# The inverse's X on the other partition half: four quarters of the array in place of two, and an order of work that has level products first

## What is computed

```
mem = 0.9 * mem + sd_t;  spike = sigmoid(10 * (mem - 0.5)) in the gradient, (mem > 0.5) in value
mem = mem - spike * 0.5
alpha = sigmoid(ab_t + alpha_spike * spike);  beta = sigmoid(bb_t + sum(spike * beta_spike))
alpha = 1 and beta = 0 where no key channel of the head spikes
s = s * alpha[:, None];  u = k_t @ s
s = s - beta * outer(k_t, u) + beta * outer(k_t, v_t)
out_t = s^T q_t
```

## Time and profile before

| | |
|---|---|
| median of 3 runs | 1183.43 us (1169.3 to 1190.45) |
| the profiled execution | 1186.2 us, span 1184.5 us |
| mean granted TensorE clock | 0.956 |
| PE busy | 1079.8 us (91%), 17266 matmuls |
| PEld busy | 769.0 us (65%) |
| DVE busy | 701.1 us (59%) |
| ACT busy | 519.5 us (44%) |
| POOL busy | 200.7 us (17%) |

### The profile page before, as it was taken

How to read it: one execution, slowest core, us unless ns; L and a number is a source line. 1 busy time by engine, 2 the same in 40 slices (tenths; PEclk the granted TensorE clock), 3 DMA queues, 4 the chain that set the end, 5 groups by cost and what they waited for, 6 DMA issues and landing times. The chain is left out here.

```text
span 1184.5 us, 41088 instructions
## 1 busy us (share of the span) xinstructions
PE 1079.8 (91%) x17266; PEld 769.0 (65%) x17266; DVE 701.1 (59%) x2517; ACT 519.5 (44%) x1500; POOL 200.7 (17%) x390
## 2 busy tenths in 40 slices
PE   7878789999999999999999997898999999899987
PEld 3332278888888888888888884456456456545642
DVE  2887868888878888887776551244336225323610
ACT  7566213444444444444444343144254245325411
POOL 7100101122122122212211201211103001110200
PEclk8999759999999999999999898899999999899999
DMA  2000000000000000000000003100000000000000
GB/s 89 1 1 1 1 2 3 5 4 4 4 4 4 4 5 4 4 4 4 4 27 4 4 4 101 31 1 1 0 9 10 1 9 1 10 1 1 10 1 9
DMA packets 12805, 11.38 MB, mean 10 GB/s; under 512 B 1563, under 2 KB 11407, under 8 KB 12623
## 3 DMA queue, kind: packets, MB, share of 16 engines
q1 hardware_dynamic: 12623, 8.75, 2.5%
HBM read 7.70 MB, written 1.05 MB: 7 GB/s over the span
## 5 line engine op out<-in xcount | busy, mean ns | idle before, releaser
L1220 ACT COPY work<-banks 128x128 f32<-128x128 f32 x160 | 42.8, 268 | 168.8 <-PE banks L926 168.8
L892 PE MATMUL banks<-work 64*64 64x64 f32 x3072 | 102.6, 232 | 6.7 <-DVE gates L599 5.8
L926 PE MATMUL banks<-work,gates 64*64 64x32 f32 x2560 | 105.3, 221 | 3.1 <-issue 2.8
L946 PE MATMUL banks<-work 64*64 64x32 f32 x2560 | 105.5, 223 | 0.4 <-ACT work L1220 0.4
L203 DVE SCALAR_TENSOR_TENSOR mom<-gates 128x16 f32<-128x16 f32 x512 | 101.3, 198 | 5.8
L926 PEld LDWEIGHTS banks<-work,gates 64*64 64x64 f32 x2560 | 93.5, 139 | 15.4 <-issue 11.4
L599 DVE COPY_PREDICATED gates<-work,banks 128x256 f32<-128x256 uint32 x192 | 101.9, 531 | 1.1
L199 DVE SCALAR_TENSOR_TENSOR gates<-mom,gates 128x16 f32<-128x16 f32 x512 | 96.7, 189 | 9.6 <-ACT gates L1193 4.5
L604 DVE TENSOR_TENSOR work<-work,banks 128x128 f32<-128x128 f32 x128 | 36.8, 288 | 101.1 <-PE banks L936 99.9
L936 PEld LDWEIGHTS banks<-work 64*64 64x64 f32 x2048 | 74.2, 139 | 32.9 <-issue 22.3
L946 PEld LDWEIGHTS banks<-work 64*64 64x64 f32 x2560 | 92.2, 139 | 0.5 <-ACT work L1220 0.5
(11 more groups left out here) (235 smaller groups left out, 2348.9 us busy)
## 6 DMA issues: line engine op xcount, KB each, us to landing
qT<-in_x_dram SPq DMA_DIRECT2D x4, 256.0 KB, 4.3
work<-in_x_dram SPq DMA_DIRECT2D x4, 256.0 KB, 4.0
out_dram<-work SPq DMA_DIRECT2D x4, 256.0 KB, 3.1
gates<-in_w_ff_dram SPq DMA_DIRECT2D x3, 256.0 KB, 3.1
wv_sb<-in_wv_dram SPq DMA_DIRECT2D x1, 512.0 KB, 4.9
work<-in_w_out_dram SPq DMA_DIRECT2D x1, 512.0 KB, 5.3
gates<-in_x_Wq_dram SPq DMA_DIRECT2D x1, 512.0 KB, 5.9
gates<-in_x_Wk_dram SPq DMA_DIRECT2D x1, 512.0 KB, 6.6
```

The source lines that it names most:

```text
L892: last = pe.matmul(level_out(l)[to, a], KS[rows, n.two, hp], late[rows, hp], start=True, stop=True)
L926: last = pe.matmul(packed(psZX, l)[rows, hp], EA[rows, n.three, l, hp], first_half(X, l)[rows, hp], start=True, stop=True)
L946: last = pe.matmul(packed(psXT, l)[rows, hp], Z[rows, l - 1, hp], second_half(XT[:, n.two], l)[rows, hp], start=True, stop=True)
L1220: ac.copy(first_half(Z[:, l - 1], l), packed(psZX, l)).then_inc(z_ok, 1)
```

## The change

X, Z, XT, EA and res of a head get places of their own (`at_x`, `at_z`, `at_xt`, `at_level`, `at_res`), such that make_z, make_x, turn_start and solve read one partition half and write either one, two heads for each quarter of the array. make_xt and read_chunk stay within a half. Matmuls from the two halves must not write one bank at once, so X's and Z's products are spread over banks 6 and 7 (`psZX = paired(6)`), and XT's products move to the second half of bank 5, where the spike counts were. The counts move to free columns of the level products' bank 0, by a matmul of their own, `spike_counts`. Since that bank is then read by alpha and beta, levels 1 and 3 wait for these, and alpha moves behind keep of level 0. make_xt waits for the ScalarE operations that read bank 5. The copy that starts XT becomes three copies (two of them move a half to the other).

The order within a step: TensorE does level ahead of xt, with spike_counts and spike_sums of l = 4 around that level (before, both were at the end of l = 3). VectorE does add_xt behind keep, and drive one place earlier.

The core of the diff (the index changes of the other matmul loops are of the kind shown for make_z; `counts`, `counts_as` and the like give the counts' place):

```diff
-        psZX, psXT = bank[6], bank[7]
+        psZX = paired(6)
+        psZX_half = psZX[:, :, 0:W]
+        psXT = psG[:, B * C:B * C + HP * W].rearrange("p (a n) -> p a n", a=HP)
...
+        def counts(g):
+            if g.n <= HP:
+                return psG[:, B * C:2 * B * C]
+            return psL[:, 0:2, 2 * C:4 * C]
...
+        by_time = [(par, 2 * t + (t + swap) % 2) for par in range(2) for swap in range(2) for t in range(2)]
+        by_parity = [(par, 2 * t + (par + swap) % 2) for t in range(2) for swap in range(2) for par in range(2)]
...
+        def at_level(par, hp):
+            return head_rows[hp // 2], 2 * par + (hp // 2 + hp) % 2
+
+        def at_x(par, hp):
+            return head_rows[hp // 2], 2 * (hp % 2) + par
+
+        def at_z(par, hp):
+            return head_rows[hp % 2], 2 * (hp // 2) + par
+
+        def at_xt(par, hp):
+            return head_rows[hp % 2], 2 * ((hp // 2 + hp) % 2) + par
+
+        def at_res(par, hp):
+            return head_rows[hp % 2], 2 * par + hp // 2
 
...
                 def alpha(g):
                     ve.wait_ge(al0_ok, g.n + 1)
-                    ve.scalar_tensor_tensor(g.tokens(aT[:, g.hp]), by_chunk(psG[:, B * C:2 * B * C]), 0.0, by_chunk(al0),
-                                            ALU.is_equal, ALU.max).then_inc(alpha_ok, 1)
+                    ve.wait_ge(count_mm, g.n + 1)
+                    ve.scalar_tensor_tensor(by_chunk_as(g, g.tokens(aT[:, g.hp])), counts_by_chunk(g), 0.0,
+                                            by_chunk_as(g, by_chunk(al0)), ALU.is_equal, ALU.max).then_inc(alpha_ok, 1)
 
                 def beta(g):
...
                             add_x(nxt, l)
                         spike(scan, h + 1)
-                        if nxt:
-                            add_xt(nxt, l)
                         spike(scan, h + 2)
                         if aft:
                             prefix(aft, l)
@@ -676,6 +713,10 @@
                         spike(scan, h + 4)
                         if aft:
                             keep(aft, l)
+                        if nxt:
+                            add_xt(nxt, l)
+                        if l == 4 and gate:
+                            drive(gate)
                         spike(scan, h + 5)
                         if l == 1 and gate:
                             spikes(gate)
@@ -683,16 +724,12 @@
                             beta(gate_old)
                         if l == 3 and aft2:
                             scale_key(aft2)
-                        if l == 4 and gate:
-                            drive(gate)
                         if l == 4 and aft2:
                             scale_query(aft2)
                     spike(scan, 6 * NINV)
                     if cur:
                         update(cur, 0)
                         update(cur, 1)
-                    if gate:
-                        alpha(gate)
                     if aft2:
                         prefix(aft2, 0)
                         suffix(aft2, 0)
@@ -700,6 +737,8 @@
                     if aft2:
                         diagonal(aft2)
                         keep(aft2, 0)
+                    if gate:
+                        alpha(gate)
                     if cur and cur.it == ROUNDS - 2:
                         scale_out()
 
...
+                def level(n, l, gate=None, gate_old=None):
+                    if l == 1 and gate_old:
+                        pe.wait_ge(alpha_ok, gate_old.n + 1)
+                    if l == 3 and gate_old:
+                        pe.wait_ge(beta_ok, gate_old.n + 1)
...
-                        for rows in head_rows:
-                            last = pe.matmul(packed(psZX, l)[rows, hp], EA[rows, n.three, l, hp], first_half(X, l)[rows, hp],
-                                             start=True, stop=True)
+                    for head in by_time:
+                        (rows, a), (_, q), (to, z) = at_level(*head), at_x(*head), at_z(*head)
+                        last = pe.matmul(packed(psZX_half, l)[to, z], EA[rows, n.three, l, a], first_half(X, l)[rows, q],
+                                         start=True, stop=True)
                     last.then_inc(z_mm, 1)
...
-                def make_xt(n, l):
+                def make_xt(n, l, gate, gate_old):
+                    if l == 1 and gate_old:
+                        pe.wait_ge(be0_ok, gate_old.n + 1)
+                    if l == 5 and gate:
+                        pe.wait_ge(zal_ok, gate.n + 1)
                     pe.wait_ge(z_ok, n.it * NINV + l)
                     if n.it or l >= 2:
                         pe.wait_ge(xt_ok, n.it * NINV + l - 1)
-                    for hp in range(HP):
-                        for rows in head_rows:
-                            last = pe.matmul(packed(psXT, l)[rows, hp], Z[rows, l - 1, hp],
-                                             second_half(XT[:, n.two], l)[rows, hp], start=True, stop=True)
+                    for head in straight:
+                        (rows, a), (_, z) = at_xt(*head), at_z(*head)
+                        last = pe.matmul(packed(psXT, l)[rows, a], Z[rows, l - 1, z],
+                                         second_half(XT[:, n.two], l)[rows, a], start=True, stop=True)
                     last.then_inc(xt_mm, 1)
 
                 def values(n):
...
+                def spike_counts(g, aft=None):
+                    if aft:
+                        pe.wait_ge(e_ok, aft.it * LEVELS + 4)
+                    if g.n:
+                        pe.wait_ge(beta_ok, g.n)
+                    pe.wait_ge(spk_ok, g.n + 1)
+                    pe.matmul(counts(g), bdones[:, :], counts_as(g, spk[:, g.two]), start=True, stop=True).then_inc(count_mm, 1)
+
...
-                    pe.matmul(psG[:, 0:B * C], wad_sb[:, g.hp, :], g.tokens(auT_all), start=True, stop=True)
-                    pe.matmul(psG[:, B * C:2 * B * C], bdones[:, :], spk[:, g.two], start=True, stop=True)\
+                    pe.matmul(psG[:, 0:B * C], wad_sb[:, g.hp, :], g.tokens(auT_all), start=True, stop=True)\
                         .then_inc(ab_mm, 1)
 
...
@@ -1057,16 +1112,20 @@
                                 read_state(cur, 1)
                         if nxt and l < NINV:
                             make_x(nxt, l)
+                        if l == 4 and gate and gate.n <= HP:
+                            spike_counts(gate)
+                        if l == 4 and gate and gate.n > HP:
+                            spike_counts(gate, aft)
+                        if aft:
+                            level(aft, l, gate, gate_old)
+                        if l == 4 and gate:
+                            spike_sums(gate)
                         if nxt:
-                            make_xt(nxt, l)
-                        if aft:
-                            level(aft, l)
+                            make_xt(nxt, l, gate, gate_old)
                         if l == 3 and cur:
                             correct(cur)
                         if l == 3 and prev:
                             turn_out(prev)
-                        if l == 3 and gate:
-                            spike_sums(gate)
...
-                    ac.copy(XT[:, n.two], EA[:, n.three, 0]).then_inc(x_init, 1)
+                    a = EA[:, n.three, 0].rearrange("p (r s) t -> p s r t", s=2)
+                    ac.copy(XT[:, n.two, 0:2], a[:, 0])
+                    for rows, other in (head_rows, head_rows[::-1]):
+                        last = ac.copy(XT[other, n.two, 2:4], a[rows, 1])
+                    last.then_inc(x_init, 1)
 
```

More of the change, by code:

```diff
@@ L603, in add_x @@
                     at_ = first_half(X, l)
[L604 removed]
+                    ve.tensor_tensor(at_, at_, packed(psZX_half, l), ALU.add).then_inc(x_ok, 1)
                 def add_xt(n, l):
@@ L898, in turn_start @@
                         pe.wait_ge(sd_ok, NSD)
+                        pe.wait_ge(qk_ok, NQ_ALL)
                     pe.wait_ge(x_init, n.it + 1)
                     pe.wait_ge(x_ok, n.it * NX)
-                    for hp in range(HP):
-                        for rows in head_rows:
-                            last = pe.matmul(x0_out[rows, hp], XT[rows, n.two, hp], eye[rows], start=True, stop=True)
+                    for head in by_time:
+                        (rows, a), (to, q) = at_xt(*head), at_x(*head)
+                        last = pe.matmul(x0_out[to, q], XT[rows, n.two, a], eye[rows], start=True, stop=True)
                     last.then_inc(x0_mm, 1)
@@ L933, in make_x @@
                         pe.wait_ge(xt_ok, n.it * NINV + l - 1)
[L934 to L937 removed]
+                    for head in by_time:
+                        (rows, a), (_, z), (to, q) = at_xt(*head), at_z(*head), at_x(*head)
+                        last = pe.matmul(packed(psZX_half, l)[to, q], XT[rows, n.two, a],
+                                         first_half(Z[:, l - 1], l)[rows, z], start=True, stop=True)
```

(30 more changed lines are left out.)

37 lines of the change are left out of this document (20 added, 17 removed).

## The result

| | before | after |
|---|---|---|
| median | 1178.28 us | 1237.18 us (1235.91 to 1240.87, 4 runs) |
| ratio to before | | 1.053, 95% interval 1.0445 to 1.0619 |
| span of the profiled execution | 1184.5 us | 1239.1 us |
| mean granted TensorE clock | 0.956 | 0.912 |

The account below looks back on a forecast made before the run. TensorE was taken to bound the chunk loop, VectorE close behind. From 1186.2 us, +13 for gated and -14 for ungated rounds made 1185; clock falls added 62: 1247 us, range 1170 to 1290.

Parts of the forecast that it names:

- the sum: Whole kernel with the clock unchanged: 1186.2 us, plus 13 in gated rounds, minus 14 in ungated ones, makes 1185 us.
- my own sign: Sign that the forecast is right: the loop's granted TensorE clock falls from 1.00 to 0.75 to 0.85.
- What a set costs: TensorE's 16-instruction sets: z, x and turn_start save 0.24 us each, solve 0.43, together 2.8 us of a 17.24 us round.
- The head: Level 0 to step 1's make_x: alpha waits behind level 0's vector work, beta_sums starts at 2.79 us, make_x 1.6 later.
- x1 to x2: From make_x of step 1 to that of step 2, which waits for add_xt: 2.57 us, 0.4 longer, TensorE idle 0.9.
- x2 to level 0: From step 2's make_x to the next level 0: 11.4 us, before 12.8, with savings partly lost to split matmul runs.
- The round: A round with scan and gate at full clock: 3.85 + 2.57 + 11.4 = 17.8 us, 0.55 more than 17.24.
- Rounds without a gate: The eight rounds without beta_sums, counts and sums: 2.2 us less for four, about 1.2 for the last four, together -14.
- The clock: TensorE's clock falls behind the new pause in 20 of 25 gated rounds, at 3.1 us each: +62 us.
- the clock holds: Rival: the loop's clock does not fall and the kernel takes 1185 us, bounds 1165 to 1205; chance 0.2.
- the wait for alpha is not in the way: Rival: alpha comes within 1.2 us of level 0, step 1's make_x does not move, 1146 us; chance 0.1.
- falls in every gated round: Rival: the clock falls in all 25 gated rounds and stays down longer, 1275 to 1300 us; chance 0.15.

Follow-up runs that it names:

- e5: The changed kernel with four unneeded 128x128 matmuls filling TensorE's pause ahead of beta_sums, which still waits for alpha; 1222.3 us, 1.035 of before.
- e10: The changed kernel, beta_sums not waiting for alpha from the sixth gate on, old order of xt, level and add_xt in all steps; 1148.9 us, 0.976 of before.
- e1: The changed kernel, but from the sixth gate on beta_sums no longer waits for alpha; 1183.7 us, 1.004 of before.
- e4: The kernel before with only the order of the steps changed: level ahead of xt, add_xt behind keep; 1213.6 us, 1.026 of before.
- e8: As e1, with keep_out ahead of start_xt on ScalarE; 1185.5 us, 1.004 of before.
- e2: The kernel before with only alpha moved, behind keep of level 0; 1362.8 us, 1.155 of before.
- e9: As e2, with the pause ahead of beta_sums filled by four 128x128 matmuls whose result nobody reads; 1225.5 us, 1.043 of before.
- e11: As e4 (old places, new order), with alpha moved behind keep of level 0; 1283.6 us, 1.085 of before.
- e12: As e10 (new places, old order), with beta_sums waiting for alpha again; 1246.3 us, 1.054 of before.
- e3: The changed kernel with alpha right behind suffix of level 0, ahead of diagonal and keep; 1191.9 us, 1.011 of before.

## Why the prediction was right, and where its terms were off

The forecast of 1247 us, +5%, came out at 1237.2. The sign and the place held: a pause of TensorE behind z1 that waits for alpha, a clock that falls in four of five rounds, and x2 waiting for add_xt. That the total came within 10 us is luck. I had the rounds at full clock as a wash (1185 us) and put the whole loss, 62 us, on the clock. The runs show the reverse: e5, at full clock, has 1222 us, so the sum was 37 us short, and the clock takes 15 to 22 us, so its term was 40 to 47 too large. The two errors offset each other. By my own sign the clock of the loop was to fall to 0.75 to 0.85; it is 0.89.

- *What a set costs.* Right: 0.25 us for the crossed sets of 32 columns. Of the 2.8 us a round that I added up from it, 1.0 is had in e10 (16.38 against 17.42), with the order taken back and without the wait for alpha.
- *The head.* Right in kind, 0.25 us short: beta_sums starts at 3.04, forecast 2.79, since prefix of level 0 waits for the two updates (0.92 after level 0, not 0.70). I had counted that wait in the last piece of the round, where it doesn't belong.
- *x1 to x2.* 2.76 us (438.58 to 441.34), forecast 2.57, with the wait for add_xt of 0.98, forecast 0.9. Right.
- *x2 to level 0.* 11.74 us, forecast 11.4. spike_counts costs 0.75: from x4 to the level behind it 1.00 (447.30 to 448.30), of which the set of x4 itself is 0.25; forecast 0.76. But the 0.43 us of solve came to little: from solve to x4 it is 0.86 (446.44 to 447.30), 0.22 of it idle, against 0.91 before. The profile puts the wait of x4's weight load down to ScalarE's copy of Z, which a shorter solve no longer covers; no run tests that.
- *The round.* At full clock 18.6 us once and 19.0 us three times, in place of 17.8: the sum was 1.2 us short, 30 us over 25 rounds. The three pieces above make 0.8 of it, the wait of x for add_xt in step 3 the rest: I had looked for it in step 2 only. It is in steps 2 and 3 of e1, e4 and e5, and e4 shows the price of the order by itself in the kernel before, 1.0 us a round.
- *Rounds without a gate.* Wrong: 15.66 us (689.53 to 705.19), forecast 13.2, before 15.4. The 14 us of gain there were not to be had: the last four distances between starts of level 0 are 71.8 us together (669.53 to 741.33), against 71.2 before, with falls of the clock in both. TensorE's timeline where it stood still in that round:

```profile
691.27 0.19 PE L970 MATMUL banks<-work,gates 64*64 64x32 f32 x1 [0.86 <-issue]
691.82 0.43 PE L980 MATMUL banks<-work 64*64 64x32 f32 x16 [0.36 <-ACT work L1283]
694.21 0.44 PE L980 MATMUL banks<-work 64*64 64x32 f32 x16 [0.67 <-DVE work L647]
...
702.33 0.55 PE L1034 MATMUL banks<-work 64*64 64x128 f32 x6 [1.00 <-DVE work L594]
```

  The 0.86 us at 691.27 have no releaser in the profile, and such idle time stands in the kernel before too (0.97 at 620.32); without them the round is 14.8 us. The wait at 694.21 was in the sum, the one of read_state (1034) not. In this round it ends with scale_query on VectorE (594, until 702.22) and ScalarE's copy (1355, until 702.18) ends with it; in e1 the copy is the last three times. I had costed start_xt's two further copies at nothing, under ScalarE's idle time; there the cover is thinner than an average says, though e8 shows that this wait alone isn't what the time hangs on.
- *The clock.* Right that it falls in most rounds with a gate: in 16 of 20, and e5 shows the pause to be the cause. Too dear: I took 3.1 us for each of 20 falls, 62 us, from two rounds of the kernel before. There x doesn't wait for add_xt, so a slower clock has less to hide behind; that is a likely reason, and only e5's 30.5 us against 11.1 speak for it. It is 15 to 22 us by e5, and 0.8 us a round by 19.73 against a mean of 18.93 of the four at full clock. In e2 it is 5.4 us a round (24.42 against e9's 18.99), 137 us. So the price taken lay between the two kernels' and fitted neither. That the clock is at 1.00 but for two places was misread too: the first three rounds of the loop have 0.73, 0.50 and 0.90 in the kernel before.
- *The rival "the clock holds"* fell by the clock alone, and would have been wrong about its time too: e5, in which it holds, has 1222 us, not 1185. *The rival "the wait for alpha is not in the way"* is e1 in effect: 1184, not 1146; with the order taken back as well it is e10, 1149. *The rival of falls in every gated round*, 1275 to 1300, fell with the four of 20 rounds that kept the full clock and with the price.

What stays open is the mechanism by which order and places change how long the clock stays down behind one and the same pause. e11 and e12 show that they do, and that neither alone accounts for it; so no price of a fall taken from one of these kernels holds for another, which is where my 62 us went wrong.

## What to carry to other kernels

A saving on the engine that is busiest is only had if what it waits for comes sooner too: here some 2.3 us of matmuls a round were to be saved (ten sets by 0.23), one vector operation moved behind five others took back as much, and a changed order of two others cost more on top. When data moves to another place, look at each wait that guarded the old place: beta_sums still waited for alpha though nothing tied them any more, and taking that out and the order back turned +5% into -2.4% (e10). And a pause of TensorE has no fixed price: 0.7 us cost the round 0.5, and one of 1.75 to 1.9 us cost the round 1.8 (after against e1), 2.2 (e11 against e4), 3.8 (e12 against e10) or 7.0 (e2 against before), by what stood around it. Waits can also hide behind a slower clock: those for add_xt were 11 us of the stretch in the changed kernel and 30 once the clock held (e5).

## What the runs showed of the hardware

- A pause of 1.75 us per 24 us round took the mean clock to 0.74 and 137 us with it; the same pause with 1.7 us of dense matmuls in it left it at 1.00. Filling brought e2 from 1362.8 to 1225.5 us, and the changed kernel from 1237.2 to 1222.3.
- A pause of 0.7 us in each round of the same kernel left the clock at 1.00, one of 0.8 us in the changed kernel (e3) at 0.99.
- A pause of 1.9 us in each round left it at 0.96 in e11, with more idle time than e2 around it.
- Sets of 16 instructions of 64x64 take 0.25 us through four quarters with 32 columns or with 64, and 0.48 through two. The Trainium skill (TensorEngine Tiling (Array Packing), Key Properties) says that tiles work independently; these rows are its size here, and a lone matmul of 128x128 by 256 columns between two such sets costs 0.75 us (447.30 to 448.30, less 0.25), 0.43 of it the matmul: the other 0.32 I put down to the drain at a change of the tiling mode, there and back, of which the same section speaks; no run takes it apart.
